# Mixture of experts: second product as three fp32r products, gelu written back into its bank, its rounded copy by ScalarE and the rest by VectorE

## The chip, the cores and the metric

The kernel runs on one core of one Trainium2 chip. The metric is the device time of one execution in microseconds (us); lower is better. "The median" is the median of the runs shown, "the profiled execution" the single one whose trace is read. Engines are named as the profile names them: PE is TensorE's matmul side, PEld its weight loads, ACT ScalarE, DVE VectorE, POOL GpSimd, SP SyncE.

## The reference, cut to what matters

The whole model is a chain of blocks on 2048 tokens of 128 features. The change touches only the mixture of experts, which runs twice, as the first and the third block:

```python
def _L0_ffn_ref(x, Wr, W1, b1, W2, b2):          # x: 8 x 256 x 128
    ...
    logits = xf @ Wr.T                            # 2048 x 8
    probs = jax.nn.softmax(logits, axis=-1)
    top_v, top_i = jax.lax.top_k(probs, TOP_K)    # TOP_K = 2
    top_v = top_v / jnp.sum(top_v, axis=-1, keepdims=True)
    comb = jnp.zeros((T, E), dtype=xf.dtype).at[jnp.arange(T)[:, None], top_i].add(top_v)
    h = jax.nn.gelu(jnp.einsum('td,efd->etf', xf, W1) + b1[:, None, :], approximate=False)
    y = jnp.einsum('etf,edf->etd', h, W2) + b2[:, None, :]
    out = jnp.einsum('etd,te->td', y, comb)
...
x = x + 0.5 * _L0_ffn_ref(_layernorm(x), ...)     # mixture of experts
x = x + _L0_attn_ref(_layernorm(x), ...)          # gated recurrence
x = x + 0.5 * _L0_ffn_ref(_layernorm(x), ...)     # mixture of experts, same weights
x = x + 0.5 * _L1_ffn_ref(_layernorm(x), ...)     # local transformer, 6 layers
x = x + _L1_attn_ref(_layernorm(x), ...)          # attention with a learned bias
x = x + 0.5 * _L1_ffn_ref(_layernorm(x), ...)     # local transformer
```

All 8 experts are computed for all tokens (hidden size 512), and the two chosen ones are picked by the weights in `comb`.

## The kernel before

The program runs the blocks one after the other, with a barrier between them: layer norm, mixture of experts (`moe_phase`), layer norm, recurrence, layer norm, `moe_phase` again, layer norm, local transformer (by far the longest), layer norm, attention, layer norm, local transformer, layer norm. Activations stay in SBUF with features on the 128 partitions and the 2048 tokens along the free axis. Order within a block is the program order on each engine, with semaphores between engines; there is no scheduler.

`moe_phase` works in 32 steps (`STEPS`): step s is expert e = s // 4 on token chunk c = s % 4 of 512 tokens. In a step:

- `hidden(s, f)` for f = 0..3: a block of 128 hidden units for the 512 tokens goes into PSUM `bank[f]`. It is one `exact_product` (lines 45 to 51): x and W1 are each kept as two fp32r tensors, a rounded "high" one and the remainder "low" one, and three fp32r matmuls (high by high, low by high, high by low) add up to an almost exact fp32 product. GpSimd splits W1 of each expert (lines 223 to 226), ScalarE and VectorE split x once.
- `gelus(s)`: ScalarE applies gelu and bias from `bank[f]` to `H` in SBUF, fp32 (line 308). It releases the bank (semaphore `gel`) for `hidden(s + 1, f)`.
- `out(s, q)` for q = 0..3: 128 tokens of the result, four plain fp32 matmuls over f with a 128x128 piece of H as the weights that are loaded and W2's 128 columns as the moving operand, into `bank[4 + q % 2]` (line 252).
- `accumulate(s, q)`: VectorE multiplies by the gate `comb` and adds into `acc` (lines 339, 342). It waits for `out(s, q)` and frees the bank of `out(s, q + 2)` (semaphore `accd`).

TensorE's order is hidden(0), hidden(1), out(0), hidden(2), out(1) and so on: `out` is one step behind. The gate chain (softmax, top 2; lines 356 to 384) runs on VectorE before its first `accumulate`. At steps 5 and 8 the gates are turned by TensorE (`turn_gates`) and copied by ScalarE; at the end `turn_sums` and `add` turn the sums back, add the second bias and add the result to the residual `M`. Weights W1, W2 and b1 are double buffered by expert and loaded by SP.

Of the kernel before, what the change touches and what calls it, by code (L numbers as in the profile page):

```python
# [12 lines left out]
P = 128  # L13
# [139 lines left out]
def moe_phase(nc, res, d, M, XN):  # L153

    bank, ident = res["bank"], res["ident"]
    with ExitStack() as ctx:
# [11 lines left out]
        w1h, w1l = sb("moe_w1h", [P, 2, FFN], FP32R), sb("moe_w1l", [P, 2, FFN], FP32R)  # L168
        w2 = sb("moe_w2", [P, 2, FFN])
        b1 = sb("moe_b1", [P, 2, FB])  # L170
        b2 = sb("moe_b2", [EXPERTS, P])
# [10 lines left out]
        combT = sb("moe_combT", [EXPERTS, NT])  # L182
        H = sb("moe_H", [P, 2, FB * CH])
        acc = sb("moe_acc", [P, TILES, P])
        ldr, lgd, dch, expd, combd = [sem("moe_" + n) for n in ("ldr", "lgd", "dch", "expd", "combd")]
        w1ld, w2ld = [[sem(f"moe_{n}{k}") for k in range(2)] for n in ("w1ld", "w2ld")]
        xhd, xld, whd, wld = [sem("moe_" + n) for n in ("xhd", "xld", "whd", "wld")]
# [13 lines left out]
        with nc.Block() as block:  # L201
            @block.sync
            def _(sp):
                sp.dma_start(wr[:, :], d["moe_wr"]).then_inc(ldr, 16)
                sp.dma_start(b2[:, :], d["moe_b2"]).then_inc(ldr, 16)
                for e in range(EXPERTS):
                    k = e % 2
                    if e >= 2:
                        sp.wait_ge(wld, e - 1)
                    sp.dma_start(w1[:, k, :], d["moe_w1"][e, :, :]).then_inc(w1ld[k], 16)  # L210
                    if e >= 2:
                        sp.wait_ge(down, (e - 1) * TILES)
                    sp.dma_start(w2[:, k, :], d["moe_w2"][e, :, :]).then_inc(w2ld[k], 16)
                    sp.dma_start(b1[:, k, :], d["moe_b1"][e, :, :]).then_inc(w2ld[k], 16)

            @block.gpsimd
            def _(pool):
                for e in range(EXPERTS):
                    k = e % 2
                    pool.wait_ge(w1ld[k], e // 2 * 16 + 16)  # L220
                    if e >= 2:
# [3 lines left out]
                    nc.gpsimd.tensor_tensor(w1l[:, k, :], w1[:, k, :], w1h[:, k, :].bitcast(FP32),  # L225
                                            ALU.subtract).then_inc(wld, 1)

            @block.tensor
            def _(pe):
# [12 lines left out]
                def out(s, q):  # L242
                    e, c = divmod(s, NC)
                    if q == 0:
                        pe.wait_ge(gel, (s + 1) * FB)
                        if c == 0:
                            pe.wait_ge(w2ld[e % 2], e // 2 * 32 + 32)
                    if 4 * s + q >= 2:
                        pe.wait_ge(accd, 4 * s + q - 1)
                    for f in range(FB):  # L250
                        o = f * CH + q * P
                        i = nc.tensor.matmul(bank[4 + q % 2][:, 0:P], H[:, s % 2, o:o + P],
                                             w2[:, e % 2, f * P:(f + 1) * P], start=(f == 0), stop=(f == FB - 1))
                    i.then_inc(down, 1)
# [44 lines left out]
            def _(act):  # L299
                def gelus(s):  # L300
# [3 lines left out]
                    if c == 0:  # L304
                        act.wait_ge(w2ld[e % 2], e // 2 * 32 + 32)
                    for f in range(FB):
                        act.wait_ge(up, s * FB + f + 1)
                        nc.scalar.activation(H[:, s % 2, f * CH:(f + 1) * CH], bank[f][:, :], ACT.Gelu,  # L308
                                             bias=b1[:, e % 2, f:f + 1]).then_inc(gel, 1)

# [14 lines left out]
            def _(dve):  # L325
# [7 lines left out]
                def accumulate(s, q):  # L333
# [6 lines left out]
                    else:  # L340
                        dve.wait_ge(accd, (s - NC) * 4 + q + 1)
                        nc.vector.scalar_tensor_tensor(out=acc[:, t, :], in0=o, scalar=comb[:, t, e:e + 1],
                                                       in1=acc[:, t, :], op0=ALU.mult, op1=ALU.add).then_inc(accd, 1)

                def add(c):
# [39 lines left out]
                dve.wait_ge(combd, 1)  # L385
                for s in range(STEPS):
                    for q in range(4):
                        accumulate(s, q)
                    if s >= STEPS - 3:
                        add(s - (STEPS - 3))  # L390
                add(3)
# [1487 lines left out]
```

## Time and profile before

| | before |
|---|---|
| median of 3 runs | 4131.73 us (4127.85 to 4132.27) |
| the profiled execution: time, span of its trace | 4129.52 us, 4127.7 us |
| mean granted TensorE clock | 0.961 of full speed |
| PE busy | 3725.9 us (90%) |
| PEld busy | 2917.0 us (71%) |
| ACT busy | 3270.4 us (79%) |
| DVE busy | 3163.1 us (77%) |
| POOL busy | 2608.6 us (63%) |
| the two mixture-of-experts blocks | about 25 to 252 us and 333 to 560 us of the span |

The busy shares are averages over blocks with different limits; the ends of matmuls are modelled, so consecutive matmuls overlap in the trace, and what counts is the distance from one start to the next. A merged row "x32" in a timeline is 32 instructions run together, from the start of the first to the end of the last. In the trace each plain fp32 matmul of the program stands as two passes (two weight loads and two matmuls); an fp32r matmul stands as one.

### The profile page before, as it was taken

The numbers are of one execution on the slowest core, as the hardware profiler recorded it, in microseconds if no ns is written. First come the engines' busy times: TensorE is split into PE (matmuls) and PEld (weight loads), VectorE is DVE, ScalarE is ACT, GpSimd is POOL, SyncE is SP. The second block draws the span as 40 slices with busy tenths as digits, with TensorE's granted clock in tenths as the row PEclk, the third lists the DMA queues.
The fourth block names the chain that finished last, engine by engine and source line by source line (L and its number), as shares of the span: only waits on it lengthen the run. The fifth ranks groups of instructions, "written<-read, shape, count | busy, mean of one in ns | idle before, by whom it ended". The sixth has DMA issues, their size and how long they took to land. (4 is left out here: it accounts for less than half of the span.)

```text
span 4127.7 us, 167239 instructions
## 1 busy us (share of the span) xinstructions
PE 3725.9 (90%) x66080; PEld 2917.0 (71%) x66080; DVE 3163.1 (77%) x6467; ACT 3270.4 (79%) x10763; POOL 2608.6 (63%) x2482
## 2 busy tenths in 40 slices
PE   8958969999999999999995886999999999999996
PEld 7947947777777777777773655777777777777773
DVE  2243248888888888888874877888888888888884
ACT  4434439998999999999982676999999999999994
POOL 0000028777777787777761647777877878777772
PEclk9988979999999999999996898999999999999998
DMA  1000013334333333333330003334333333333341
GB/s 39 19 1 24 19 43 112 118 103 120 99 111 118 105 120 96 112 117 106 120 91 8 1 1 115 117 104 120 107 103 119 102 113 113 103 120 97 111 119 37
DMA packets 547030, 361.36 MB, mean 88 GB/s; under 512 B 32320, under 2 KB 532816, under 8 KB 546000
## 3 DMA queue, kind: packets, MB, share of 16 engines
q1 hardware_dynamic: 546256, 350.66, 28.4%
q8 instruction: 532, 8.72, 0.9%
q14 instruction: 242, 1.98, 0.2%
HBM read 248.59 MB, written 101.97 MB: 85 GB/s over the span
## 5 line engine op out<-in xcount | busy, mean ns | idle before, releaser
L1285 POOL TENSOR_TENSOR lt_t<-lt_t,lt_rn 128x512 f32<-128x512 f32 x768 | 786.5, 1045 | 666.2 <-DVE lt_rn L1140 664.6
L1016 ACT ACTIVATE lt_pb<-lt_pb,lt_mx 128x64 f32<-128x64 f32 x3072 | 1022.4, 342 | 0.0
L1279 POOL TENSOR_TENSOR lt_t<-lt_t 128x512 f32<-128x512 f32 x768 | 972.1, 1287 | 12.1 <-DVE lt_t L1114 12.0
L49 PE MATMUL ps<-lt_wh,lt_xh 128*128 128x512 f32 (+1 forms) x1536 | 578.5, 377 | 83.2 <-POOL lt_xl L1258 57.9
L1016 ACT ACTIVATION_READ_ACCUMULATOR lt_pb<-lt_pb,lt_mx 128x1 f32 x3072 | 598.9, 195 | 0.0
L996 ACT ACTIVATE lt_qkT<-ps 128x512 f32<-128x512 f32 x768 | 459.4, 598 | 132.8 <-PE ps L816 132.6
L1125 DVE TENSOR_REDUCE lt_ss<-lt_sq 128x8 f32<-128x512 f32 x768 | 520.3, 678 | 41.2 <-ACT lt_sq L991 35.6
L1114 DVE TENSOR_TENSOR lt_t<-ps,lt_tab 128x512 f32<-128x512 f32 x768 | 526.0, 685 | 4.3 <-issue 1.4
L1120 DVE TENSOR_TENSOR lt_t<-ps,lt_tab 128x512 f32<-128x512 f32 x768 | 522.6, 680 | 4.0 <-PE ps L816 2.5
L51 PE MATMUL ps<-lt_wh,lt_xl 128*128 128x512 f32 (+1 forms) x1536 | 521.1, 339 | 0.0
L816 PE MATMUL ps<-ident,lt_t 128*128 128x128 f32 x3072 | 478.8, 278 | 46.1 <-ACT lt_qkT L996 41.6
L50 PE MATMUL ps<-lt_wl,lt_xh 128*128 128x512 f32 (+1 forms) x1536 | 520.2, 339 | 0.0
L991 ACT ACTIVATE lt_sq<-ps 128x512 f32<-128x512 f32 x768 | 452.7, 589 | 29.4 <-PE ps L51 28.7
L816 PEld LDWEIGHTS ps<-ident,lt_t 128*128 128x128 f32 x3072 | 356.7, 141 | 163.7 <-issue 105.3
L874 PEld LDWEIGHTS ps<-lt_pT,lt_vw 64*64 64x64 f32 x24576 | 395.6, 135 | 85.1 <-issue 84.9
L874 PE MATMUL ps<-lt_pT,lt_vw 64*64 64x32 f32 x24576 | 438.2, 221 | 0.7 <-issue 0.7
L1291 POOL TENSOR_TENSOR lt_pb<-lt_pb,lt_rd 128x512 f32<-128x512 f32 x384 | 402.0, 1047 | 26.6 <-DVE lt_rd L1157 26.5
L49 PEld LDWEIGHTS ps<-lt_wh,lt_xh 128*128 128x128 f32 x1536 | 290.2, 189 | 166.8 <-POOL lt_xl L1258 59.6
L888 PE MATMUL ps<-lt_oT,lt_wo 128*128 128x256 f32 x1536 | 402.4, 385 | 1.4 <-ACT lt_oT L1028 1.4
L1163 DVE COPY lt_vv<-ps 128x512 f32<-128x512 f32 x384 | 264.0, 688 | 170.5 <-PE ps L51 170.2
L844 PEld LDWEIGHTS ps<-lt_qkT 64*32 64x32 f32 x24576 | 268.4, 105 | 131.5 <-issue 107.6
L308 ACT ACTIVATE moe_H<-ps,moe_b 128x512 f32<-128x512 f32 x256 | 171.5, 690 | 222.5 <-PE ps L51 222.5
(213 smaller groups left out, 7462.9 us busy)
## 6 DMA issues: line engine op xcount, KB each, us to landing
lt_vw<-v_scratch SPq DMA_DIRECT2D x768, 256.0 KB, 3.7
v_scratch<-lt_vv SPq DMA_DIRECT2D x384, 256.0 KB, 2.1
lt_wraw<-in_lt_wqkv SPq DMA_DIRECT2D x56, 384.0 KB, 6.0
moe_w<-in_moe_w SPq DMA_DIRECT2D x32, 256.0 KB, 2.9
lt_wo<-in_lt_wo SPq DMA_DIRECT2D x48, 128.0 KB, 3.9
lt_w<-in_lt_w SPq DMA_DIRECT2D x12, 341.0 KB, 4.3
lt_w<-in_lt_w SPq DMA_DIRECT2D x12, 192.0 KB, 3.6
lt_gl<-in_lt_qs SPq DMA_DIRECT2D x2, 768.0 KB, 7.1
```

Of the source, the lines that this page charges most:

```text
L49: nc.tensor.matmul(out, lh, rh, start=start, stop=False)
L50: nc.tensor.matmul(out, lh, rl, start=False, stop=False)
L51: return nc.tensor.matmul(out, ll, rh, start=False, stop=stop)
L816: ins = nc.tensor.transpose(TB[:, q * P:(q + 1) * P], t1[:, u[1] % 2, t, q * P:(q + 1) * P], ident[:, :])
L874: ins = nc.tensor.matmul(OR[r][64 * e:64 * e + 64, t * P + w * WIN:t * P + w * WIN + WIN], vw[h, k, 4 * t + w, e * DH:(e + 1) * DH], pT[h, ...
L996: nc.scalar.activation(qkT[:, u[1] % 2, :, WIN + t * P:WIN + (t + 1) * P], TB.rearrange("p (a n) -> p a n", a=4), ACT.Copy).then_inc(tE[t], 1)
L1016: ins = nc.scalar.activation(p, p, ACT.Exp, bias=mx[:, par, c:c + 1], accum_out=sm[:, par, c:c + 1])
L1114: nc.vector.tensor_tensor(o4, a4[:, :, :, ::-1, :], s4, ALU.mult).then_inc(rotd[t], 1)
L1120: nc.vector.tensor_tensor(t1[:, u[1] % 2, t, :].rearrange("p (w h c) -> p w h c", w=2, c=DH), A[t][:, :].rearrange("p (w h c) -> p w h c", ...
L1125: nc.vector.tensor_reduce(ss[:, u[1] % 2, 8 * t:8 * t + 8], sq[:, t, :].rearrange("p (h c) -> p h c", c=DH), AX.X, ALU.add).then_inc(ssd[t ...
L1279: nc.gpsimd.tensor_tensor(o, o, t2[:, t, :], ALU.add).then_inc(padd[t], 1)
L1285: nc.gpsimd.tensor_tensor(o, o, rn[:, u[1] % 2, 8 * t:8 * t + 8].unsqueeze(2).to_broadcast([P, 8, DH]), ALU.mult).then_inc(qkd[t], 1)
```

## The change

The second product gets the same treatment as the first. W2 is split on GpSimd into `w2h` and `w2l`. Gelu writes back into its own PSUM bank; a second ScalarE instruction copies the bank, rounded to fp32r, to `Hh` (it waits for the gelu's own completion); VectorE subtracts `Hh` from the bank and writes `Hl`, and only this now signals `gel`, which frees the bank for the next `hidden` and H for `out`. Each matmul of `out` becomes three fp32r matmuls with 128 moving columns. VectorE's order is written anew: the four `low` of step 0 come after the gate chain, and from then on `low` of step s is woven between `accumulate` of step s - 1. b1 has semaphores of its own and waits for gelu; W2's load waits for the split of W2 and no longer for `out`.

```diff
--- before.py
+++ after.py
@@ -167,6 +167,7 @@
         w1 = sb("moe_w1", [P, 2, FFN])
         w1h, w1l = sb("moe_w1h", [P, 2, FFN], FP32R), sb("moe_w1l", [P, 2, FFN], FP32R)
         w2 = sb("moe_w2", [P, 2, FFN])
+        w2h, w2l = sb("moe_w2h", [P, 2, FFN], FP32R), sb("moe_w2l", [P, 2, FFN], FP32R)
         b1 = sb("moe_b1", [P, 2, FB])
         b2 = sb("moe_b2", [EXPERTS, P])
         wr = sb("moe_wr", [P, EXPERTS])
@@ -180,10 +181,11 @@
         m2 = sb("moe_m2", [P, TILES])
         den = sb("moe_den", [P, TILES])
         combT = sb("moe_combT", [EXPERTS, NT])
-        H = sb("moe_H", [P, 2, FB * CH])
+        Hh, Hl = sb("moe_Hh", [P, 2, FB * CH], FP32R), sb("moe_Hl", [P, 2, FB * CH], FP32R)
         acc = sb("moe_acc", [P, TILES, P])
         ldr, lgd, dch, expd, combd = [sem("moe_" + n) for n in ("ldr", "lgd", "dch", "expd", "combd")]
-        w1ld, w2ld = [[sem(f"moe_{n}{k}") for k in range(2)] for n in ("w1ld", "w2ld")]
+        w1ld, w2ld, b1ld = [[sem(f"moe_{n}{k}") for k in range(2)] for n in ("w1ld", "w2ld", "b1ld")]
+        w2hd, w2d, geld, high = [sem("moe_" + n) for n in ("w2hd", "w2d", "geld", "high")]
         xhd, xld, whd, wld = [sem("moe_" + n) for n in ("xhd", "xld", "whd", "wld")]
         up, gel, down, accd = [sem("moe_" + n) for n in ("up", "gel", "down", "accd")]
         turned, turnedE, whole, added = [sem("moe_" + n) for n in ("turned", "turnedE", "whole", "added")]
@@ -209,9 +211,11 @@
                         sp.wait_ge(wld, e - 1)
                     sp.dma_start(w1[:, k, :], d["moe_w1"][e, :, :]).then_inc(w1ld[k], 16)
                     if e >= 2:
-                        sp.wait_ge(down, (e - 1) * TILES)
+                        sp.wait_ge(w2d, e - 1)
                     sp.dma_start(w2[:, k, :], d["moe_w2"][e, :, :]).then_inc(w2ld[k], 16)
-                    sp.dma_start(b1[:, k, :], d["moe_b1"][e, :, :]).then_inc(w2ld[k], 16)
+                    if e >= 2:
+                        sp.wait_ge(geld, (e - 1) * TILES)
+                    sp.dma_start(b1[:, k, :], d["moe_b1"][e, :, :]).then_inc(b1ld[k], 16)
 
             @block.gpsimd
             def _(pool):
@@ -224,6 +228,13 @@
                     pool.wait_ge(whd, e + 1)
                     nc.gpsimd.tensor_tensor(w1l[:, k, :], w1[:, k, :], w1h[:, k, :].bitcast(FP32),
                                             ALU.subtract).then_inc(wld, 1)
+                    pool.wait_ge(w2ld[k], e // 2 * 16 + 16)
+                    if e >= 2:
+                        pool.wait_ge(down, (e - 1) * TILES)
+                    nc.gpsimd.tensor_copy(w2h[:, k, :], w2[:, k, :]).then_inc(w2hd, 1)
+                    pool.wait_ge(w2hd, e + 1)
+                    nc.gpsimd.tensor_tensor(w2l[:, k, :], w2[:, k, :], w2h[:, k, :].bitcast(FP32),
+                                            ALU.subtract).then_inc(w2d, 1)
 
             @block.tensor
             def _(pe):
@@ -244,13 +255,14 @@
                     if q == 0:
                         pe.wait_ge(gel, (s + 1) * FB)
                         if c == 0:
-                            pe.wait_ge(w2ld[e % 2], e // 2 * 32 + 32)
+                            pe.wait_ge(w2d, e + 1)
                     if 4 * s + q >= 2:
                         pe.wait_ge(accd, 4 * s + q - 1)
                     for f in range(FB):
                         o = f * CH + q * P
-                        i = nc.tensor.matmul(bank[4 + q % 2][:, 0:P], H[:, s % 2, o:o + P],
-                                             w2[:, e % 2, f * P:(f + 1) * P], start=(f == 0), stop=(f == FB - 1))
+                        w = slice(f * P, (f + 1) * P)
+                        i = exact_product(nc, bank[4 + q % 2][:, 0:P], (Hh[:, s % 2, o:o + P], Hl[:, s % 2, o:o + P]),
+                                          (w2h[:, e % 2, w], w2l[:, e % 2, w]), start=(f == 0), stop=(f == FB - 1))
                     i.then_inc(down, 1)
 
                 def turn_gates(half):
@@ -302,11 +314,12 @@
                     if s >= 2:
                         act.wait_ge(down, (s - 1) * 4)
                     if c == 0:
-                        act.wait_ge(w2ld[e % 2], e // 2 * 32 + 32)
+                        act.wait_ge(b1ld[e % 2], e // 2 * 16 + 16)
                     for f in range(FB):
                         act.wait_ge(up, s * FB + f + 1)
-                        nc.scalar.activation(H[:, s % 2, f * CH:(f + 1) * CH], bank[f][:, :], ACT.Gelu,
-                                             bias=b1[:, e % 2, f:f + 1]).then_inc(gel, 1)
+                        nc.scalar.activation(bank[f][:, :], bank[f][:, :], ACT.Gelu, bias=b1[:, e % 2, f:f + 1]).then_inc(geld, 1)
+                        act.wait_ge(geld, s * FB + f + 1)
+                        nc.scalar.activation(Hh[:, s % 2, f * CH:(f + 1) * CH], bank[f][:, :], ACT.Copy).then_inc(high, 1)
 
                 for c in range(NC):
                     nc.scalar.activation(xh[:, cols(c)], XN[:, cols(c)], ACT.Copy).then_inc(xhd, 1)
@@ -342,6 +355,12 @@
                         nc.vector.scalar_tensor_tensor(out=acc[:, t, :], in0=o, scalar=comb[:, t, e:e + 1],
                                                        in1=acc[:, t, :], op0=ALU.mult, op1=ALU.add).then_inc(accd, 1)
 
+                def low(s, f):
+                    h = slice(f * CH, (f + 1) * CH)
+                    dve.wait_ge(high, s * FB + f + 1)
+                    nc.vector.tensor_tensor(Hl[:, s % 2, h], bank[f][:, :], Hh[:, s % 2, h].bitcast(FP32),
+                                            ALU.subtract).then_inc(gel, 1)
+
                 def add(c):
                     m = M[:, cols(c)]
                     dve.wait_ge(whole, c + 1)
@@ -383,11 +402,22 @@
                 link(nc.vector.tensor_tensor(eq[:, :, :], eq[:, :, :], bc(m2[:, :]), ALU.mult))
                 nc.vector.tensor_tensor(comb[:, :, :], one1[:, :, :], eq[:, :, :], ALU.add).then_inc(combd, 1)
                 dve.wait_ge(combd, 1)
-                for s in range(STEPS):
-                    for q in range(4):
-                        accumulate(s, q)
-                    if s >= STEPS - 3:
-                        add(s - (STEPS - 3))
+                for f in range(FB):
+                    low(0, f)
+                for s in range(1, STEPS):
+                    low(s, 0)
+                    low(s, 1)
+                    accumulate(s - 1, 0)
+                    accumulate(s - 1, 1)
+                    low(s, 2)
+                    accumulate(s - 1, 2)
+                    low(s, 3)
+                    accumulate(s - 1, 3)
+                    if s >= STEPS - 2:
+                        add(s - (STEPS - 2))
+                for q in range(4):
+                    accumulate(STEPS - 1, q)
+                add(2)
                 add(3)
         clear(nc, sems)
 
```

What the new order looks like. First VectorE from the end of the gate chain on, before (names: `moe_acc` the sums, `moe_comb` the gates, `ps` PSUM, `M` the residual):

```order
30 L383 TENSOR_TENSOR moe_eq<-moe_eq,moe_m_2 128x128 [waits moe_dch_2]
31 L384 TENSOR_TENSOR moe_comb<-moe_one_2,moe_eq 128x128 [waits moe_dch_2]
32 L339 TENSOR_SCALAR moe_acc<-ps,moe_comb 128x128 [waits moe_down_2,moe_combd_2]
33 L339 TENSOR_SCALAR moe_acc<-ps,moe_comb 128x128 [waits moe_down_2] x15
34 L342 SCALAR_TENSOR_TENSOR moe_acc<-ps,moe_comb,moe_acc 128x128 [waits moe_accd_2,moe_down_2] x104
```

The same place with the change (L403 is the last of the gate chain, L361 is `low`, L352 `accumulate`):

```order
31 L403 TENSOR_TENSOR moe_comb<-moe_one_2,moe_eq 128x128 [waits moe_dch_2]
32 L361 TENSOR_TENSOR moe_Hl<-ps,moe_Hh 128x512 [waits moe_high_2,moe_combd_2]
33 L361 TENSOR_TENSOR moe_Hl<-ps,moe_Hh 128x512 [waits moe_high_2] x5
34 L352 TENSOR_SCALAR moe_acc<-ps,moe_comb 128x128 [waits moe_down_2] x2
35 L361 TENSOR_TENSOR moe_Hl<-ps,moe_Hh 128x512 [waits moe_high_2]
36 L352 TENSOR_SCALAR moe_acc<-ps,moe_comb 128x128 [waits moe_down_2]
37 L361 TENSOR_TENSOR moe_Hl<-ps,moe_Hh 128x512 [waits moe_high_2]
38 L352 TENSOR_SCALAR moe_acc<-ps,moe_comb 128x128 [waits moe_down_2]
```

`low` of step 0 stands behind the whole gate chain, where before nothing that TensorE's second `hidden` waits for did; per step there are now four instructions of 128x512 more.

ScalarE at its first steps, before:

```order
11 L308 ACT_TABLE_LOAD [waits moe_up_2]
12 L308 ACTIVATE moe_H<-ps,moe_b_2 128x512 [waits moe_w2ld0_2]
13 L308 ACTIVATE moe_H<-ps,moe_b_2 128x512 [waits moe_up_2] x7
14 L308 ACTIVATE moe_H<-ps,moe_b_2 128x512 [waits moe_up_2,moe_down_2]
```

and with the change (L320 gelu, L322 the rounded copy):

```order
11 L320 ACT_TABLE_LOAD [waits moe_up_2]
12 L320 ACTIVATE ps<-ps,moe_b_2 128x512 [waits moe_b1ld0_2]
13 L322 ACTIVATE moe_Hh<-ps 128x512 [waits moe_geld_2]
14 L320 ACTIVATE ps<-ps,moe_b_2 128x512 [waits moe_up_2]
15 L322 ACTIVATE moe_Hh<-ps 128x512 [waits moe_geld_2]
```

Each gelu is followed by a copy that waits for it; no table load stands between them.

## Rows read from the trace of the kernel before

**Rows 1.** The page: its head
```profile
span 4127.7 us, 167239 instructions
```

**Rows 2.** Window of a block: its us; busy PE PEld DVE ACT POOL; clock, DMA
```profile
25.00:252.00 227.00, 222.12 (x1497) 201.36 (x1498) 56.56 (x160) 91.43 (x138) 15.05 (x16) 0.97 0.07 20
```

**Rows 3.** Timeline of PE, one step: start us, us, instruction, count
```profile
124.96 3.73 PE L252 MATMUL ps<-moe_w,moe_H 128*128 128x128 f32 x32
128.45 0.48 PE L49 MATMUL ps<-moe_xh,moe_w1h 128*128 128x512 f32 x1
...
131.29 3.73 PE L252 MATMUL ps<-moe_w,moe_H 128*128 128x128 f32 x32
```

**Rows 4.** Timelines of ACT and DVE, the same step, idle before in brackets
```profile
129.48 2.70 ACT L308 ACTIVATE moe_H<-ps,moe_b 128x512 f32<-128x512 f32 x4 [3.64 <-PE ps L51]
132.38 0.35 DVE L342 SCALAR_TENSOR_TENSOR moe_acc<-ps,moe_comb,moe_acc 128x128 f32<-128x128 f32 x1 [3.30 <-PE ps L252]
```

**Rows 5.** Timeline of PE in the attention block: 64 moving columns, 128-column loads
```profile
2249.26 7.09 PE L1501 MATMUL ps<-fa_w,fa_hb 128*128 128x64 f32 x32 [2.06 <-ACT fa_hb L1465]
...
2264.74 3.79 PE L1501 MATMUL ps<-fa_w,fa_hb 128*128 128x64 f32 x32 [0.61 <-ACT fa_hb L1465]
```

**Rows 6.** Windows: inside the second stretch, and after a later idle; columns as Rows 2
```profile
2264.80:2268.30 3.50, 3.50 (x32) 3.50 (x32) 3.50 (x6) 0.62 (x2) 2.39 (x2) 1.00 0.00 0
2271.20:2276.30 5.10, 5.10 (x32) 5.10 (x33) 4.52 (x8) 1.51 (x3) 2.41 (x2) 0.68 0.01 3
```

**Rows 7.** Weight loads by line: duration ns min/median/max; the columns loaded stand last
```profile
L1605 PEld LDWEIGHTS ps<-fa_pT,fa_vv x768: 106/109/110, 2310.8 to 2451.7; 128*32 128x32 f32 x192
L1501 PEld LDWEIGHTS ps<-fa_w,fa_hb x192: 186/192/338, 2249.3 to 2299.5; 128*128 128x128 f32 x192
L51 PEld LDWEIGHTS ps<-lt_wh,lt_xl x1536: 187/188/331, 598.6 to 4045.2; 128*128 128x128 f32 x192
```

**Rows 8.** Timeline of PE in the local transformer: fp32r with 256 moving columns
```profile
1018.66 0.28 PE L50 MATMUL ps<-lt_wl,lt_xh 128*128 128x256 f32 x1
1018.78 0.28 PE L51 MATMUL ps<-lt_wh,lt_xl 128*128 128x256 f32 x1
```

**Rows 9.** Page and timeline rows: PSUM copy, subtract, self-waits on ACT, the split on POOL
```profile
L996 ACT ACTIVATE lt_qkT<-ps 128x512 f32<-128x512 f32 x768 | 459.4, 598 | 132.8 <-PE ps L816 132.6
L1114 DVE TENSOR_TENSOR lt_t<-ps,lt_tab 128x512 f32<-128x512 f32 x768 | 526.0, 685 | 4.3 <-issue 1.4
...
640.91 0.20 ACT L1002 ACTIVATE lt_y<-lt_vm 128x16 f32<-128x16 f32 x1
641.14 0.31 ACT L1005 ACTIVATE lt_y<-lt_y,ln 128x16 f32<-128x16 f32 x1
...
131.59 0.61 POOL L223 CAST moe_w1h<-moe_w 128x512 fp32r<-128x512 f32 x1 [23.37 <-PE ps L51]
132.28 1.27 POOL L225 TENSOR_TENSOR moe_w1l<-moe_w,moe_w1h 128x512 fp32r<-128x512 f32 x1
```

**Rows 10.** Timelines at the start of both blocks
```profile
38.13 0.39 PE L49 MATMUL ps<-moe_xh,moe_w1h 128*128 128x512 f32 x1
...
35.29 1.28 ACT L308 ACT_TABLE_LOAD   x1 [0.57 <-PE ps L51]
...
41.10 0.29 DVE L384 TENSOR_TENSOR moe_comb<-moe_one,moe_eq 128x128 f32<-128x128 f32 x1
...
349.20 0.29 DVE L384 TENSOR_TENSOR moe_comb<-moe_one,moe_eq 128x128 f32<-128x128 f32 x1
...
40.88 3.73 PE L252 MATMUL ps<-moe_w,moe_H 128*128 128x128 f32 x32
348.58 3.62 PE L252 MATMUL ps<-moe_w,moe_H 128*128 128x128 f32 x31
...
34.57 0.63 PE L51 MATMUL ps<-moe_xh,moe_w1l 128*128 128x512 f32 x1
35.00 0.63 PE L49 MATMUL ps<-moe_xh,moe_w1h 128*128 128x512 f32 x1
```

## Prediction

> **What bounds the kernel now.** The page comes first: a span of 4127.7 us [rows 1]. The profiled execution took 4129.52 us, 2.2 us under the median of 4131.73 us that the forecast is set against; differences are added to the median. The change touches only the two mixture-of-experts blocks, so next comes the window over the first one [rows 2]: in 227 us TensorE is busy for 222, ScalarE for 91, VectorE for 57, GpSimd for 15, at a clock of 0.97. The other block is the same code. TensorE alone sets the time here, and the question is what the new matmuls cost on it, and whether the others still fit beside it.
>
> The timeline of one step [rows 3] gives the unit. The 16 plain products of `out` stand as 32 passes, started from 124.96 to 128.45 us: 3.49 us. The 12 fp32r matmuls of `hidden` take from 128.45 to 131.29: 2.84 us. A step is 6.33 us, and 32 steps twice are 405 us. ScalarE works 2.70 us of it and then waits 3.64 for TensorE, VectorE waits 3.30 [rows 4].
>
> **The second product, on the path.** Removed: 32 passes of 128 columns. Added: 48 fp32r matmuls of 128 columns. Passes within a run of 32 start (3.73 - 0.275) / 31 = 0.1115 us apart, the 0.275 being one matmul's own modelled length (as in [rows 8], 0.28). What will an fp32r one take? No row shows fp32r with 128 moving columns. With 512 it starts every 2.84 / 12 = 0.237 us, joints included [rows 3], with 256 every 0.12 [rows 8]: time goes with the columns, and 128 would make 0.06, were streaming all. But each matmul here also loads 128 columns of weights, and this has a price of its own. The rows that show it are L1501 of the attention block: 64 moving columns in a plain fp32 pass, which stream half as long as 128 would (the passes of 128 columns take 0.11), and still 32 of them need 3.79 us, (3.79 - 0.275) / 31 = **0.1134 us** each [rows 5], at full clock, 1.00 [rows 6]. At the half level (1.2 GHz) the same run needs 7.09 us, 0.213 each with 0.48 for the last one [rows 5]. So it is the load that paces them. Is the load of fp32r quicker? Its duration is 187 ns against 192 for plain fp32, both for 128 columns, and 109 for 32 columns [rows 7]: it grows with the columns, by some 0.85 ns each, 109 ns for 128, and the fp32r load lies on the same line. Every line of `exact_product` shows its own load, also where the weights are those of the matmul before, so all 48 pay it.
>
> I take 0.1134, the row with the same number of loaded columns and the same streaming time as an fp32r matmul of 128 (half of a plain pass). `out` becomes 48 x 0.1134 less the 0.08 us that a joint with `hidden` saves (32 x 0.1115 = 3.57 against 3.49): 5.36 us, **1.87 us more per step, 64 steps: +120 us**. The lower bound is the average of today's passes, 3.49 / 32 = 0.109: 5.24, +1.75, +112 us. The upper one is the pace of fp32r with 256 columns, 0.117 over the run it is part of, which the two rows give as 0.12: 5.54, +2.05, +131 us. The step is then 8.2 us.
>
> A rule of the skill speaks for the same thing. The Trainium skill, "TensorE: Matmul & The Clock Gate", section "LDWEIGHTS (loading the stationary operand)", gives a load as its columns over 1.2, an estimate of 107 ns for 128, whatever the rows; the trace agrees, with 109 to 113, and by it alone the 48 loads are 5.14 us, +1.65 a step, +105 us.
>
> **ScalarE and VectorE, beside the path.** A gelu keeps its 0.67 us (2.70 / 4). The copy out of PSUM costs 0.60 (as L996) [rows 9], and its wait for the gelu's completion some 0.03, as between two small dependent instructions there (640.91 + 0.20 to 641.14) [rows 9]. A pair makes 1.3 us, four of them 5.2 of 8.2: hidden, with 3 us to spare. VectorE gets four subtractions of 0.69 (as L1114, which also reads PSUM) [rows 9] beside four accumulations of 0.35: 4.2 us. The chain through both, from the start of `hidden(s, 0)`: first gelu after 1.03 us (128.45 to 129.48 [rows 3, 4]), pairs end at 2.3, 3.6, 4.9 and 6.2, the low parts at 3.0, 4.3, 6.8 (behind the second accumulate, at 5.8) and 8.2 (behind the third). `hidden(s + 1, 2)` and `(s + 1, 3)` want these banks at 9.6 and 10.3, `out(s)` starts at 11.0. The accumulates end 0.6 us or more before `out` wants their bank. No wait for TensorE. These edits cost nothing as long as TensorE needs over 5.7 us a step; the spare is what covers them.
>
> **GpSimd, SP and the DMAs.** The split of W2 is 0.61 + 1.27 us per expert [rows 9], beside the same for W1, in 33 us of four steps: nothing. At the start it stands between the splits of experts 0 and 1, ready some 8 us before `out(0)`. W2's load leaves earlier than before; the load of b1 now waits for gelu, and behind it on SP stands W1 of the next expert, which then has three steps, 24 us, for a transfer and a split of a few us. Nothing.
>
> **The start of each block.** This is a new wait. Before, `hidden(1, 0)` followed `hidden(0, 3)` at once, at 38.13, and `out(0)` began at 40.88. Now `hidden(1, f)` wants `low(0, f)`, and VectorE does these behind the gate chain, which ends at 41.10 + 0.29 [rows 10]. The gelu pairs, from the end of the table load at 36.6 on [rows 10], are done by 41.8, so VectorE decides: 42.1, 42.8, 43.5, 44.2. At full clock `out(0)` starts at 44.9, 4.0 us late. But TensorE has been idle since `hidden(0, 3)`, nearly 4 us, and an idle of 1.3 us was followed by a fall to the half level in the run after it (clock 0.68 in that window) [rows 6]. The first products of the block ran at half level too, 0.43 us apart (34.57, 35.00). Then the 12 of `hidden(1)` need 5.1 us from 42.1, `out(0)` starts at 47.2, 6.3 late. In the second block the chain ends at 349.49 and `out(0)` stood at 348.58 [rows 10]: 4.4 late, or 6.7. I take the half level, **+13 us** for both; lower bound 8.4; upper bound 24, if `out(0)` too stays at half level in each block (+5.4 us each).
>
> **The sum.** 4131.7 + 120 + 13 = **4265 us**. Its bounds: +112 + 8 gives 4252, +131 + 24 gives 4287. A difference of 0.2%, 8 us, is about what a measurement of this kernel can tell from none.
>
> **Rivals.** *Faster: the load is not what paces fp32r.* Then a matmul goes with its columns, 0.061 us (half of [rows 8]), `out` needs 48 x 0.061 - 0.08 = 2.85, 0.64 less than now; 64 steps give -41, the start +13: 4104 us. The change wins below 0.070 us a matmul, (3.57 - 13 / 64) / 48. In favour: the sum of streamed columns does fall by a quarter, 48 x 128 against 32 passes at two cycles a column. Against: [rows 5, 7]. Chance 0.07, values between 0.061 and 0.105 included.
> The Trainium skill has rules for this rival: in the same page, section "Weight-path perf modes", loads of 128 columns are fast where the type is not FP32, which could be read to take in fp32r. By it the time would be this rival's; the trace disagrees, with 187 ns for fp32r beside 192 for fp32.
>
> *The clock falls.* The new `out` streams only half the time, and TensorE could drop to 1.2 GHz in it: 48 x 0.213 = 10.2 us, `hidden` staying at 2.84: 13.1 a step, +6.7 x 64 = +430 us, about 4575; with `hidden` at half level too 15.3, about 4720. For: at half level the L1501 run of 7 us did not lift it [rows 5]. Against: the run of 3.5 us at full level stayed at 1.00 [rows 6], and `hidden` comes back every 8 us. Chance 0.05.
>
> *fp32r below 256 columns costs as much as a plain product.* 2 x 0.109 = 0.218 each, `out` 10.4, +6.9 x 64 + 13: about 4590. For: nothing in this kernel uses it below 256, so nothing shows that it doesn't. Against: 256 columns go at 0.12. Chance 0.06.
>
> *ScalarE becomes the bound*, by a table load before each gelu and each copy, 1.28 us as at the block's start [rows 10]: 4 x (1.3 + 2 x 1.28) = 15.4 us a step, near 4720. Decides from 2.0 us a pair. Against: the built order has none. Chance 0.02.
>
> **How the numbers follow.** The forecast has 0.80; its own range is 4252 to 4287, widened to 4240 and 4300 for what the bounds leave out (the phase of the clock at the ends of the blocks, joints of 12 matmuls). The rivals' 0.20 lie outside. Faster: 0.05 out of the first rival; same: 0.01; slower: 0.94.
>
> **What would show it.** Right: `out`'s 48 matmuls 5.2 to 5.5 us from first to last start, loads of 128 columns near 0.11 us apart, steps of 8.2 us, PE never idle in steps 2 to 31, clock 1.00 there; an idle of about 4 us on PE after `hidden(0)` in both blocks, ended by `moe_Hl`; both blocks together 120 to 155 us longer and nothing else changed. Wrong: a pace under 0.1 us (the faster rival), a clock below 1.00 inside steps, a matmul pace near 0.21 at full clock, or TensorE waiting for `moe_Hl` in every step.

## The result, and the profile after

| | before | after |
|---|---|---|
| median of 4 runs each | 4130.69 us (4127.85 to 4132.27) | 4268.92 us (4263.55 to 4271.36) |
| the profiled execution: time, span | 4129.52 us, 4127.7 us | 4271.36 us, 4269.6 us |
| mean granted TensorE clock | 0.961 | 0.957 |

The ratio is 1.0334, with a 95% interval of 1.0316 to 1.0352: the change is slower by 3.3%. The forecast was 4265 us, 4240 to 4300.

All matmuls of `exact_product` stand on lines 49 to 51, so the tiles tell `out` from `hidden`. Timeline of PE after the change, from the first to the last matmul of one `out` and the `hidden` on both sides; columns as [rows 3]:

```profile
143.55 0.45 PE L49 MATMUL ps<-moe_xh,moe_w1h 128*128 128x512 f32 x1
...
146.40 0.23 PE L49 MATMUL ps<-moe_w2h,moe_Hh 128*128 128x128 f32 x1
146.46 0.28 PE L50 MATMUL ps<-moe_w2l,moe_Hh 128*128 128x128 f32 x1
...
151.60 0.28 PE L51 MATMUL ps<-moe_w2h,moe_Hl 128*128 128x128 f32 x1
151.71 0.45 PE L49 MATMUL ps<-moe_xh,moe_w1h 128*128 128x512 f32 x1
```

`hidden` takes 2.85 us as before, `out` 146.40 to 151.71, which is 5.31 us against 3.49 [rows 3]: 1.82 us more, and the step is 8.16 us against 6.33. The second to the last of its 48 matmuls start 5.14 / 46 = 0.1117 us apart. From the first to the second it is only 0.06. The reading is that the first one's weights were loaded under the last matmul of `hidden`, so that only its 128 streamed columns hold up the next, and that every later one waits for a load; e1 and e2b below test it. The loads themselves (duration in nanoseconds: least, median, most) last as long as those of [rows 7]:

```profile
L50 PEld LDWEIGHTS ps<-moe_w2l,moe_Hh x1024: 187/192/193, 47.0 to 683.6; 128*128 128x128 f32 x171
```

ScalarE and VectorE in the same step, for [rows 4]:

```profile
144.56 0.66 ACT L320 ACTIVATE ps<-ps,moe_b 128x512 f32<-128x512 f32 x1 [3.29 <-PE ps L51]
145.26 0.60 ACT L322 ACTIVATE moe_Hh<-ps 128x512 fp32r<-128x512 f32 x1
145.75 0.66 ACT L320 ACTIVATE ps<-ps,moe_b 128x512 f32<-128x512 f32 x1
```
```profile
149.50 0.68 DVE L361 TENSOR_TENSOR moe_Hl<-ps,moe_Hh 128x512 fp32r<-128x512 f32 x1
```

A pair of gelu and copy recurs every 1.19 us, with no table load in it, and ScalarE still waits 3.29 us a step for TensorE. Inside the steps TensorE waits for nobody, as this window shows (columns as [rows 2]): busy 230.00 of 230.00, clock 1.00.

```profile
60.00:290.00 230.00, 230.00 (x1699) 214.91 (x1698) 111.44 (x225) 133.99 (x228) 22.75 (x24) 1.00 0.04 13
```

At the start of the block stands the new wait. Timelines of PE and of VectorE there, for [rows 10]:

```profile
42.02 0.76 PE L49 MATMUL ps<-moe_xh,moe_w1h 128*128 128x512 f32 x1 [4.36 <-DVE moe_Hl L361]
...
43.44 0.63 PE L49 MATMUL ps<-moe_xh,moe_w1h 128*128 128x512 f32 x1
43.87 0.63 PE L50 MATMUL ps<-moe_xl,moe_w1h 128*128 128x512 f32 x1
...
47.02 0.22 PE L49 MATMUL ps<-moe_w2h,moe_Hh 128*128 128x128 f32 x1
```
```profile
40.86 0.29 DVE L403 TENSOR_TENSOR moe_comb<-moe_one,moe_eq 128x128 f32<-128x128 f32 x1
41.19 2.48 DVE L361 TENSOR_TENSOR moe_Hl<-ps,moe_Hh 128x512 fp32r<-128x512 f32 x4
```

The gate chain ends, the four low parts follow, `hidden(1)` starts after an idle of 4.36 us and at the half level (0.43 us from start to start), `out(0)` at 47.02.

One block can be cut into three pieces: from its first expert matmul to the first of `out(0)`, from there to the last pair of turned sums (`turn_sums(2)` and `(3)`, lines 272 and 274 before, 284 and 286 after), and from these to the first matmul of the next layer norm (L83). These are the ends of block 1, PE's timeline, before and then after:

```profile
33.58 0.77 PE L49 MATMUL ps<-moe_xh,moe_w1h 128*128 128x512 f32 x1
...
244.14 1.12 PE L272 MATMUL ps<-moe_combT,moe_b 8*128 8x512 f32 x2
...
251.64 5.37 PE L83 MATMUL ps<-M,avg 128*128 128x512 f32 x8 [3.15 <-PEq L127]
```
```profile
33.09 0.77 PE L49 MATMUL ps<-moe_xh,moe_w1h 128*128 128x512 f32 x1
...
308.19 1.12 PE L284 MATMUL ps<-moe_combT,moe_b 8*128 8x512 f32 x2
...
311.01 2.07 PE L284 MATMUL ps<-moe_combT,moe_b 8*128 8x512 f32 x2
313.02 2.08 PE L286 MATMUL ps<-ident,moe_acc 128*128 128x128 f32 x8
318.31 6.08 PE L83 MATMUL ps<-M,avg 128*128 128x512 f32 x8 [3.22 <-PEq L127]
```

| piece | block 1 before, after | block 2 before, after | both |
|---|---|---|---|
| start, to `out(0)` | 7.30, 13.93 | 6.90, 13.70 | +13.4 |
| steps, to the last sums | 203.26, 261.17 | 203.26, 261.17 | +115.8 |
| end, to the layer norm | 7.50, 10.12 | 7.14, 10.34 | +5.8 |
| the block | 218.06, 285.22 | 217.30, 285.21 | +135.1 |

The spans differ by 141.9 us. The layer norms behind the blocks hold another 1.2 (from L83 to their L87 5.20 us before, 5.92 and 5.66 after). The last 5.6 us lie in code that the change leaves alone. Between profiled executions of the kernels below, the time behind block 2, whose code is the same in all, lies between 3558.8 and 3575.8 us, so 5.6 us there needs no cause in the change, and none is shown. For that reason the experiments are read in two numbers: the median, and the two blocks together.

The third row of the table was not foreseen. Windows at the end of block 1, after the change:

```profile
306.00:309.00 3.00, 3.00 (x23) 2.40 (x21) 0.70 (x2) 0.00 (x0) 0.00 (x0) 1.00 0.00 0
309.00:312.00 3.00, 3.00 (x10) 2.05 (x10) 0.69 (x1) 0.00 (x0) 0.00 (x0) 0.59 0.00 0
312.00:315.00 3.00, 3.00 (x10) 1.78 (x8) 0.00 (x0) 0.00 (x0) 0.00 (x0) 0.50 0.00 0
```

The clock falls to the half level (1.2 GHz) at about 309 us. The last matmuls of `hidden` lie some 13 us back there; since then PE has done `out(30)`, turned sums, `out(31)` and turned sums, never idle. The last sums take 2.07 and 2.08 in the rows above, where their first two matmuls at full clock took 1.12, and the layer norm begins at the half level. Before the change it was still at 1.00 over its last sums:

```profile
245.00:248.00 3.00, 3.00 (x17) 1.93 (x17) 0.69 (x1) 0.00 (x0) 0.00 (x0) 1.00 0.00 0
```

The profiled execution of experiment e2 had a mean granted clock of 0.55 and took 5829.82 us, against a median of 4123.56 us, so its kernel ran again as e2b, and the trace read below is that of e2b.

### The profile page after: what moved, and what is told of

It reads as the page before. It is cut to its first block and busy times, and to the rows that moved or that the text cites. A ratio compares the mean times of both kernels' runs of the same rounds, so it can differ in the third digit from the quotient of the medians.

```text
span 4269.6 us, 169855 instructions
## 1 busy us (share of the span) xinstructions
PE 3859.3 (90%) x67104; PEld 3041.6 (71%) x67104; DVE 3334.7 (78%) x6723; ACT 3399.5 (80%) x11019; POOL 2635.6 (62%) x2514
## 5 line engine op out<-in xcount | busy, mean ns | idle before, releaser
L320 ACT ACTIVATE ps<-ps,moe_b 128x512 f32<-128x512 f32 x256 | 168.9, 660 | 210.1 <-PE ps L51 210.1
```

## Experiments

The theory: a second product of 48 fp32r matmuls is paced by the load of 128 columns of weights, and this makes nearly all of the loss; the rest is the start of the block. The rivals: the streaming or the type sets the pace, or ScalarE's and VectorE's new work does. In all, "the two blocks" is the sum of both from the first expert matmul to the next L83: 435.4 us before, 570.4 after.

### e1 and e2: half the streamed columns, half the loaded ones

```diff
 # e1: W2's first 64 columns only
-w = slice(f * P, (f + 1) * P)
-i = exact_product(nc, bank[4 + q % 2][:, 0:P], (Hh[..., o:o + P], Hl[..., o:o + P]), ...)
+w = slice(f * P, f * P + 64)
+i = exact_product(nc, bank[4 + q % 2][:, 0:64], (Hh[..., o:o + P], Hl[..., o:o + P]), ...)
 # e2, e2b: 64 of H's columns as weights, W2's 128 streamed
+i = exact_product(nc, bank[4 + q % 2][0:64, 0:P], (Hh[..., o:o + 64], Hl[..., o:o + 64]), ...)
```

The accumulation follows the half that is there, and VectorE clears the sums once at the start.

> Each of the 48 matmuls of out streams 64 columns of W2 and not 128, with the same 128-column loads (half of the output is left out). If the weight load paces them, they still start 0.111 us apart, a step stays at 8.16 us and the time near 4269 us. If streaming paces them, the pace halves to about 0.056, a step is 5.5 us and the time near 4100. If the thinner stream lets TensorE's clock fall, steps at half level cost 13 us and more, and the time passes 4500.

> Each of the 48 matmuls of out loads 64 columns of H and streams the same 128 columns (half of the output is left out). If the load paces them, the pace falls to that of 64 columns loaded or 128 streamed, 0.054 to 0.061 us; out takes 2.6 to 2.9 us, a step 5.5 to 5.8, the time 4100 to 4120 us. If fp32r has a fixed price per matmul below 256 columns, or streaming sets the pace, it stays at 0.111 and 4269.

Measured: e1 4422.48 us (4413.01 to 4428.35), ratio 1.0711, 1.0693 to 1.073; the two blocks 726.3 us. e2 4123.56 us, ratio 0.998, 0.997 to 0.9989. PE's timeline in e1, in a stretch at full clock:

```profile
153.91 0.19 PE L49 MATMUL ps<-moe_w2h,moe_Hh 128*128 128x64 f32 x1
153.94 0.27 PE L50 MATMUL ps<-moe_w2l,moe_Hh 128*128 128x64 f32 x1
154.05 0.28 PE L51 MATMUL ps<-moe_w2h,moe_Hl 128*128 128x64 f32 x1
```

The pace is 0.11 us with half the stream: nothing was gained, so streaming does not set it. Only behind the first matmul does the shorter stream show: the second follows after 0.03, where with 128 streamed columns it was 0.06. But the time rose by 154 us over the changed kernel, and this is the clock. Windows of e1, over most of block 1 and over two pieces of it:

```profile
60.00:390.00 330.00, 330.00 (x1882) 298.35 (x1881) 112.49 (x244) 141.79 (x239) 22.62 (x24) 0.75 0.03 9
...
148.00:150.00 2.00, 2.00 (x16) 2.00 (x16) 0.88 (x2) 0.00 (x0) 0.00 (x0) 0.77 0.00 0
150.00:152.00 2.00, 2.00 (x6) 1.61 (x6) 0.28 (x1) 0.43 (x1) 0.00 (x0) 0.50 0.00 0
```

The profile has TensorE busy all the time, yet its mean clock is 0.75, where the changed kernel has 1.00 in its steps. In the step at 148 us the clock falls after 5 us of matmuls that load 128 columns and stream 64, and is back at full level some 3 us into the next stretch of 512-column matmuls; other steps lose it at other points, and some not at all. The rival "the clock falls" of the prediction exists, then, half a streamed width away from this change.

The mirror image, e2b:

> The same kernel as e2, run again for a profile at the full clock: the second product's matmuls load 64 columns of H and stream 128 of W2, so that half of the output's rows are left out. If the load of the stationary piece sets their pace, 48 of them take 0.055 to 0.065 us each (2.6 to 3.1 us) in place of 0.111 each (5.3 us), and the step is 5.5 to 5.9 us against 8.15. The rival (streaming sets the pace) expects 0.109 each and a step of 8.1 us, and a time near 4265.

Measured: 4118.20 us (4116.09 to 4125.06, 8 runs), ratio 0.9971, 0.996 to 0.9981; the two blocks 427.0 us. PE's timeline:

```profile
144.84 0.22 PE L49 MATMUL ps<-moe_w2h,moe_Hh 128*64 128x128 f32 x1
...
146.22 0.22 PE L51 MATMUL ps<-moe_w2h,moe_Hl 128*64 128x128 f32 x1
146.55 0.27 PE L49 MATMUL ps<-moe_w2h,moe_Hh 128*64 128x128 f32 x1
...
148.04 0.44 PE L49 MATMUL ps<-moe_xh,moe_w1h 128*128 128x512 f32 x1
```

Half the loaded columns, and the matmul takes 1.38 / 23 = 0.060 us in place of 0.1117. The load paces the second product; the type and the stream do not. (The 0.060 is at most the price of 64 loaded columns: 128 streamed ones cost as much, and e2b can't tell the two apart.) The step is 6.00 us and not 5.5 to 5.9, since with `out` this short the others come into view: at 146.22 TensorE waits 0.27 us for the bank of `out(s, 2)`, which VectorE frees only after a low part.

```profile
145.55 0.69 DVE L362 TENSOR_TENSOR moe_Hl<-ps,moe_Hh 128x512 fp32r<-128x512 f32 x1 [0.49 <-ACT moe_Hh L323]
146.16 0.67 DVE L356 SCALAR_TENSOR_TENSOR moe_acc<-ps,moe_comb,moe_acc 64x128 f32<-64x128 f32 x2
```

### e3 and e4: the matmuls alone, the side work alone

```diff
 # e3: no low part; out uses Hh in both places, gelu writes Hh as before
-(Hh[:, s % 2, o:o + P], Hl[:, s % 2, o:o + P])
+(Hh[:, s % 2, o:o + P], Hh[:, s % 2, o:o + P])
 # e4: copy and low part kept, out a plain product again
-i = exact_product(nc, bank[4 + q % 2][:, 0:P], (Hh[...], Hl[...]), (w2h[...], w2l[...]), ...)
+i = nc.tensor.matmul(bank[4 + q % 2][:, 0:P], Hh[:, s % 2, o:o + P].bitcast(FP32), w2[:, e % 2, w], ...)
```

> The matmul part alone: gelu writes its rounded value straight into Hh, no second copy, no VectorE subtraction, VectorE's order as before; the third product reads Hh in place of Hl, so the low part of H is left out. If TensorE's 48 loads are the cost and the side chain costs nothing in the steps: no wait at the start, steps of 8.16 us, 4130.7 + 64 x 1.83 + about 6.6 at the ends of the blocks = 4254 us. If the side chain had a part in the steps: shorter steps than 8.16, under 4240.

> The side chain alone: gelu in place, rounded copy, VectorE's low part and its new order, W2 split, but out is again 16 plain fp32 products of Hh and W2 (the low part of H is left out of the sum). If the side chain costs only the wait at the start: steps of 6.33 us and 12 to 13 us in all, 4143 us. If ScalarE's 4.7 us or the woven VectorE order binds once TensorE needs only 6.33 us a step: TensorE waits for moe_Hl in each step, 4160 us and more.

Measured: e3 4252.76 us (4245.89 to 4257.42), ratio 1.0301, 1.0285 to 1.0317; the two blocks 555.4 us, +120.0. e4 4151.62 us (4146.61 to 4155.27), ratio 1.0057, 1.0042 to 1.0072; the two blocks 452.4 us, +17.0. Together that is +137 for the +135 of the whole change: the parts add up, and the matmuls are seven eighths of it. For e3 4254 us was expected, for e4 4143; e4's blocks hold 13.1 us more at their starts, as expected, and the rest in small parts: 1.9 in the steps, 2.0 at the ends. In e4 the steps are 6.36 us against 6.33, so the side work is hidden even in the short step, and the wait at the start is the same as in the changed kernel:

```profile
42.09 0.76 PE L49 MATMUL ps<-moe_xh,moe_w1h 128*128 128x512 f32 x1 [4.43 <-DVE moe_Hl L362]
```

The median of e4 rose by 22 us, 5 more than its blocks; its profiled execution has 3575.8 us behind block 2, 7 more than that of before, in the range told above.

### e5: the first low parts inside the gate chain

```diff
 link(nc.vector.tensor_tensor(eq[:, :, :], lg[:, :, :], bc(m2[:, :]), ALU.is_equal))
+low(0, 0)
 ...
 dve.wait_ge(combd, 1)
-for f in range(FB):
-    low(0, f)
```

`low(0, 1)` to `low(0, 3)` stand a few instructions further on, each where the chain would wait for itself anyway.

> The changed kernel with low(0, f) placed inside the gate chain, where each is ready, not behind it. hidden(1, 0) can start near 38.6 us and not 42.0; the pairs on ScalarE then set the pace (1.19 us each), out(0) starts near 43 and not 47.0. If the start costs what the prediction says, half of it from waiting and a third from the half-level clock: 8 to 10 us less, near 4260. If the clock falls all the same in the short waits: 4 us less.

Measured: 4253.35 us (4250.49 to 4256.25), 15.6 under the changed kernel, or 13 by the ratios to before; ratio 1.0302, 1.0285 to 1.0319; the two blocks 565.0 us, 5.4 less than the changed kernel. PE's timeline:

```profile
38.90 0.47 PE L49 MATMUL ps<-moe_xh,moe_w1h 128*128 128x512 f32 x1 [1.54 <-DVE moe_Hl L361]
...
43.82 0.22 PE L49 MATMUL ps<-moe_w2h,moe_Hh 128*128 128x128 f32 x1
```

The wait falls from 4.36 to 1.54 us (three of 0.3 to 0.5 us follow it), the clock stays at the full level behind it (0.23 us from start to start, where the changed kernel has 0.43), and `out(0)` starts 3.2 us earlier. So the order on VectorE made the wait, and behind the shorter wait the half level stayed away. The two start pieces are 5.6 us shorter together, which is less than the 8 to 10 expected. Of the 15.6 us in the median the blocks show 5.4; the profiled execution has 3558.8 us behind block 2, the least of all, and why that unchanged code varies so is open.

### e7: twelve more matmuls before the last `out`

```diff
+pe.wait_ge(gel, STEPS * FB)
+for f in range(FB):
+    exact_product(nc, bank[f][:, :], (w1h[...], w1l[...]), (xh[:, cols(3)], xl[:, cols(3)]))   # result unused
 for q in range(4):
     out(STEPS - 1, q)
```

> The changed kernel with 12 more fp32r matmuls of 512 columns (their result unused) between out(30) and out(31), where no hidden stands. If it is two outs in a row, weight-bound and streaming half the time, that let the clock fall at the end of each block: the clock stays 1.00 through the turned sums, their 3.3 us a block come back, 2.8 are spent, the time stays near 4268. If the turned sums themselves bring it down: it falls all the same, and the time is 5.6 us longer, near 4275.

Measured: 4269.09 us (4261.95 to 4272.74), ratio 1.0336, 1.0319 to 1.0353; the two blocks 572.8 us. End of block 1, windows of e7 (its last sums begin at 311.10 us, where those of the changed kernel begin at 308.19):

```profile
309.00:312.00 3.00, 3.00 (x22) 2.32 (x21) 0.70 (x2) 0.00 (x0) 0.00 (x0) 1.00 0.00 0
312.00:315.00 3.00, 3.00 (x14) 1.97 (x14) 0.69 (x1) 0.00 (x0) 0.00 (x0) 0.90 0.00 0
```

With the added matmuls between the two `out`, the clock falls only in the last of the turned sums, and in block 2 behind them: the end pieces are 8.43 and 7.56 us against 10.12 and 10.34. That gives back 4.5 us, the 24 unused matmuls cost some 5.6 (24 x 0.233), and the time is the same: the remedy is worth nothing. Nor is the cause shown. PE of e3 does at the end of its blocks what PE of the changed kernel does, without the added matmuls, and in block 1 its last sums all ran at the full level:

```profile
303.69 1.12 PE L284 MATMUL ps<-moe_combT,moe_b 8*128 8x512 f32 x2
```

That end piece is 7.56 us, while the one of block 2 is 10.25, as in the changed kernel. And in e5 and e7 the clock also fell once before, in block 1, during the first turned sums, with a `hidden` only 7 us back (mean clock 0.57 from 290 to 294 us in e7), which cost some 1.6 us each time. So the point at which the clock falls moves from block to block. Two blocks with the added matmuls agree with the guess that two `out` in a row bring it down, and are too few to show it.

### e6 and e8: the other way round, W2 loaded and H streamed

If the load is the price, the second product should load W2 (one piece for 512 tokens) and stream H: 12 matmuls of 512 columns a step, like `hidden`. The result then comes transposed, as the block needs it in the end, so the turned sums go; but the gates must be spread along the columns, by one matmul of a selector with the turned gates.

```diff
-i = exact_product(nc, bank[4 + q % 2][:, 0:P], (Hh[...], Hl[...]), (w2h[..., w], w2l[..., w]), ...)
+i = exact_product(nc, bank[4 + s % 2][:, :], (w2h[..., w], w2l[..., w]), (Hh[..., h], Hl[..., h]), ...)
+nc.tensor.matmul(bank[6 + s % 2][:, :], sel[:, e, :], combT[:, cols(c)], start=True, stop=True)
+nc.scalar.activation(G[:, s % 2, :], bank[6 + s % 2][:, :], ACT.Copy)
+nc.vector.scalar_tensor_tensor(out=tmp[...], in0=bank[4 + s % 2][:, :], scalar=b2[:, e:e + 1],
+                               in1=G[:, s % 2, :], op0=ALU.add, op1=ALU.mult)
+nc.vector.tensor_tensor(m, m, tmp[...], ALU.add)
 # e8 against e6
-combT = sb("moe_combT", [40, NT], FP32R)
-sel = sb("moe_sel", [40, EXPERTS, P], FP32R)
+combT = sb("moe_combT", [P, NT], FP32R)
+sel = sb("moe_sel", [P, EXPERTS, P], FP32R)
 # cut: GpSimd builds sel before it splits any weights, and splits expert 1's only behind the gates
```

Both have `low(0, f)` inside the gate chain, as e5.

> The second product turned round: pieces of W2 are the loaded weights, H's 512 columns stream, 12 fp32r matmuls and not 48, output with features on partitions; gates are spread over the partitions by one fp32r matmul of 512 columns per step, ScalarE copies them out of PSUM, VectorE adds b2, multiplies and adds into M; acc and the turned sums at the end go. low(0, f) early. If the load paced the 48 matmuls, 12 with 512 columns take 2.8 us, a step 5.9 us, 64 x 0.4 less than before, and some 8 us less at the end of each block: 4085 to 4105, faster than before. If ScalarE (5.2 us a step) or VectorE in its new order binds: steps over 6.2 us, 4120 and more.

Measured: e6 4122.34 us (4117.56 to 4128.37, 10 runs), ratio 0.9983, 0.9974 to 0.9992; the two blocks 426.5 us. Expected was 4085 to 4105; two things ate the gain. The first stands in each step. PE's timeline of e6:

```profile
142.31 0.40 PE L51 MATMUL ps<-moe_xh,moe_w1l 128*128 128x512 f32 x1
142.64 0.50 PE L294 MATMUL ps<-moe_combT,moe_sel 40*128 40x512 f32 x1
143.07 0.50 PE L49 MATMUL ps<-moe_Hh,moe_w2h 128*128 128x512 f32 x1
143.40 0.39 PE L50 MATMUL ps<-moe_Hl,moe_w2h 128*128 128x512 f32 x1
```

From start to start it is 0.23 us, and around the matmul over 40 rows 0.33, 0.43 and 0.33. The second stands at the start of the block, on VectorE, here with what GpSimd did beside its slowest instruction:

```profile
37.29 0.64 DVE L400 TENSOR_TENSOR moe_eq<-moe_eq,rank 128x128 f32<-128x128 f32 x1
37.96 0.29 DVE L401 TENSOR_REDUCE moe_den<-moe_eq 128x16 f32<-128x128 f32 x1
38.28 1.00 DVE L402 TENSOR_TENSOR moe_one<-moe_eq,moe_den 128x128 f32<-128x128 f32 x1
```
```profile
37.87 1.27 POOL L232 TENSOR_TENSOR moe_w1l<-moe_w,moe_w1h 128x512 fp32r<-128x512 f32 x1
```

GpSimd builds the selector and splits expert 1's weights until 41.1 us, and until then VectorE's operations with two SBUF inputs take 0.58 to 1.00 us for 0.29, while the reductions, with one, keep 0.29. Each slow one ends some 0.14 us behind an instruction of GpSimd: the one of 1.00 us at 39.28, GpSimd's subtraction at 39.14. The Trainium skill, "SBUF — State Buffer", section "SBUF: two separate sides", says as much: VectorE and GpSimd share a pair of ports, one has it for a whole instruction, and two SBUF inputs on VectorE count among the cases, against an instruction of GpSimd that reads SBUF. This trace agrees, with the numbers above; GpSimd's casts and subtractions there read SBUF. e8 takes both away.

> The kernel of e6, with the selector and the transposed gates laid out on all 128 rows (rows that carry nothing are zero), the selector built by GpSimd before it splits expert 0's weights, and GpSimd's split of expert 1 held back until the gates are done. It computes the whole output. If the matmul over 40 rows is what cost 0.6 us at each gate spread, the spread matmul now runs at the pace of the others (0.23 to 0.24 us), the step is 13 matmuls of 0.233 out and the rest hidden, some 5.85 us against 6.20 in e6, so 64 steps give back 20 to 24 us; and with GpSimd idle during the gates, VectorE's operations of 128x128 there go back to 0.29 us from up to 1.0. Together 4090 us (4080 to 4105). The rival: the joint comes from the change of weights and banks, not from the number of rows. Then the step stays at 6.2 us and the time falls only by the start of the block, to 4110 to 4120.

Measured: e8 4093.02 us (4087.82 to 4094.69), before on the same chip 4129.99; ratio 0.9907, 0.989 to 0.9923; the two blocks 396.9 us, 38.5 less than before the change. PE's timeline of e8, and the instruction that took 1.00 us in e6 on VectorE's:

```profile
144.13 0.40 PE L51 MATMUL ps<-moe_xh,moe_w1l 128*128 128x512 f32 x1
144.36 0.40 PE L295 MATMUL ps<-moe_combT,moe_sel 128*128 128x512 f32 x1
144.59 0.39 PE L49 MATMUL ps<-moe_Hh,moe_w2h 128*128 128x512 f32 x1
```
```profile
36.47 0.29 DVE L403 TENSOR_TENSOR moe_one<-moe_eq,moe_den 128x128 f32<-128x128 f32 x1
```

Three times the rows, at 0.23 us: the joint came from the change in the number of rows. The step is 25 matmuls at 0.233, 5.83 us, against 6.21 in e6; the wait before `hidden(1)` is 1.28 us, with three of 0.3 to 0.5 behind it, for the low parts inside the gate chain. This version beats both kernels: 0.9% under before, 4.1% under the change (4093.02 / 4268.92). It replaces the same plain product by the same three fp32r products, and loads the other operand. It also leaves out the turned sums, adds a gate matmul to each step and has the early low parts; in the steps alone it takes 5.83 us against the 8.16 of the change.

## Why the prediction was right

**The second product.** The prediction took the pace of a matmul with 64 streamed columns, in another block and another type, for that of fp32r with 128: 0.1134 us. It is 0.1117, `out` is 5.31 us and not 5.36, and the steps cost 115.8 us where 120 was forecast, between the bounds of 112 and 131. The argument, that the load of 128 columns paces it whatever the type, is shown from both sides: e1 halves the stream and keeps 0.11, e2b halves the load and gets 0.060, e8 streams 512 columns for each load and is faster than before.

**Beside the path.** ScalarE's pair is 1.19 us, forecast 1.3, VectorE's subtraction 0.68, forecast 0.69, and TensorE is busy 230.00 of 230.00 us beside them. e4 shows that they are still hidden in a step of 6.36 us, and e2b where the cover begins to fail, at 6.0.

**The start.** Forecast 42.1 for `hidden(1)` at the half level, `out(0)` at 47.2, +13 for both blocks; measured 42.02, 47.02, +13.4. In e5 the shorter wait left the clock at its full level, so the two parts of this term (the wait and the clock that falls in it) hang together as the prediction had them. A short idle can go either way, though: 1.54 us in e5 brought no fall, 1.3 us in [rows 6] did. (In its upper bound the +5.4 us for `out(0)` at the half level is its time doubled; by the prediction's own pace of 0.213 it would be 10.2 - 5.36, +4.9. That would move the bound by 1 us.)

**The end.** This term was missing. The prediction left "the phase of the clock at the ends of the blocks" to the width of its range and gave it no price: the clock falls there, 5.8 us in the end pieces and 1.2 in the layer norms. It could have been asked: two `out` with their sums and no `hidden` between them are 13 us of little but matmuls paced by their loads, and [rows 5] held a run of such matmuls at the half level. Why the clock falls where it does is open (e3, e7). The step term, 4 us too high, hid a part of this, so it is in part luck that 4265 lies as close to 4268.92 as it does.

**The rivals.** That the load does not pace: excluded by e1 and e2b, and the faster rival with it. That the clock falls inside the steps: not here (1.00), though it does in e1, with half the streamed columns. That fp32r under 256 columns costs as much as a plain product would have meant 0.218 a matmul: it is 0.1117. A table load before each gelu or copy: none.

## What to carry to other kernels

In these runs a matmul costs the dearer of its load and its stream: about 0.11 us for 128 loaded columns, at most 0.06 for 64, 0.06 for 128 streamed in fp32r and 0.23 for 512. By these prices three fp32r matmuls can't beat the two passes of a plain fp32 product at 128 streamed columns, where each of the five takes 0.11; they gain where the stream is long against the load, as in e8 (12 x 0.233, 2.80 us, for the 3.49 of `out` before). So first choose which operand is loaded, then the type. And when a change makes a product stream less, look at the granted clock of its stretches too (0.75 on the mean in e1), above all of the last ones before a barrier.

## What was not expected of the hardware

- A busy TensorE can lose its clock. In e1 it is busy 330.00 of 330.00 us at a mean granted clock of 0.75, with 64 columns streamed per 128 loaded; at the end of the changed kernel's blocks it falls from 1.00 to 0.50 while never idle. Busy means here that the modelled times of the matmuls leave no gap. What the chip goes by these runs don't tell.
- A matmul over 40 rows between ones over 128 costs 0.3 us more at its two joints, and 0.1 at the next one (e6); over 128 rows nothing (e8).
- VectorE's small operations with two SBUF inputs took two to three and a half times as long beside GpSimd (0.58 to 1.00 us for 0.29, e6).
- The same code behind block 2 took 3558.8 to 3575.8 us in the profiled executions of ten kernels. Its cause is open.
